# Two ways to bring the expert layer's output back to its tokens: scattered by token as it is made, or stored by slot and gathered at the end

## What is computed

```python
logits = flat @ router_w
_, topk_idx = top_k(logits + router_bias, K)            # K = 4 of E = 64 experts
topk_scores = softmax(logits) at topk_idx, divided by their sum
comb[token, topk_idx] = topk_scores
g = silu(einsum('nd,edf->nef', flat, wg))               # F = 64
u = einsum('nd,edf->nef', flat, wu)
routed = einsum('ne,nef,efd->nd', comb, g * u, wd)
shared = silu(flat @ swg) * (flat @ swu) @ swd          # the shared network, hidden width 512
return routed + shared
```

## Time and profile before

| | us |
|---|---|
| median of 3 runs (lowest, highest) | 1531.79 (1531.74, 1532.27) |
| the profiled execution, first to last instruction | 1770.5 |
| PE busy in it | 1348.5 (76%) |
| VectorE busy | 1091.4 (62%) |
| GpSimd busy | 921.4 (52%) |
| ACT busy | 687.1 (39%) |

### The profile page before, as it was taken

How to read it: one execution, slowest core, us unless ns; L and a number is a source line. 1 busy time by engine, 2 the same in 40 slices (tenths; PEclk the granted TensorE clock), 3 DMA queues, 4 the chain that set the end, 5 groups by cost and what they waited for, 6 DMA issues and landing times. The chain is left out here.

```text
span 1770.5 us, 24406 instructions
## 1 busy us (share of the span) xinstructions
PE 1348.5 (76%) x7408; PEld 924.2 (52%) x7408; DVE 1091.4 (62%) x2773; ACT 687.1 (39%) x1466; POOL 921.4 (52%) x1063
## 2 busy tenths in 40 slices
PE   6686656788699986998688985638876777777775
PEld 2344523455588873564456564325544555555533
DVE  5899755556366662473777775725654655555558
ACT  5998201111366652424133613111214444544420
POOL 3999364554555546656636032663453555555520
PEclk9898577889899998999799997869888888888878
DMA  9800531121788876112111003521136444443168
GB/s 363 343 1 0 201 136 56 71 86 61 207 276 265 271 250 185 57 46 69 39 53 39 3 1 128 219 101 49 68 97 185 148 140 140 140 134 105 40 238 272
DMA packets 109395, 233.81 MB, mean 132 GB/s; under 512 B 21543, under 2 KB 43470, under 8 KB 108756
## 3 DMA queue, kind: packets, MB, share of 16 engines
q1 hardware_dynamic: 81076, 164.03, 27.6%
q0 software_dynamic: 27648, 68.23, 11.3%
q10 hardware_dynamic: 544, 0.00, 0.0%
HBM read 125.44 MB, written 115.11 MB: 136 GB/s over the span
## 5 line engine op out<-in xcount | busy, mean ns | idle before, releaser
L882 POOL DMA_INDIRECT slots_x<-arena,slot x256 | 258.2, 1009 | 207.7 <-DVEq L981 131.4
L1248 POOL DMA_INDIRECT pairs_y<-arena x192 | 189.1, 985 | 177.2 <-DVE arena L1319 117.4
L1167 PE MATMUL moe_narrow<-arena 128*128 128x128 f32 x1536 | 232.7, 301 | 8.0 <-DVE arena L1311 6.7
L1311 DVE TENSOR_TENSOR arena<-arena,moe_narrow 64x128 f32<-64x128 f32 x384 | 111.6, 291 | 205.2 <-ACT arena L1215 186.3
L1167 PEld LDWEIGHTS moe_narrow<-arena 128*128 128x128 f32 x1536 | 212.9, 215 | 16.7 <-issue 15.0
L1156 PE MATMUL moe_narrow<-ident,arena 128*128 128x128 f32 x768 | 137.7, 308 | 92.8 <-ACT arena L1209 68.3
L707 PE MATMUL moe_wide<-arena 128*128 128x512 f32 x384 | 190.7, 644 | 22.0 <-DVE arena L1002 22.0
L1209 ACT ACTIVATE arena<-moe_narrow 128x512 f32<-128x512 f32 x192 | 114.6, 597 | 197.7 <-remote 117.8
L456 POOL DMA_INDIRECT arena<-slots_y,slot x128 | 128.7, 1005 | 87.0 <-DMA arena<-slots_y,slot 46.6
L1156 PEld LDWEIGHTS moe_narrow<-ident,arena 128*128 128x128 f32 x768 | 93.7, 155 | 146.8 <-issue 143.8
L799 ACT ACTIVATE arena<-moe_wide 128x512 f32<-128x512 f32 x48 | 28.7, 598 | 319.0 <-PE moe_wide L707 153.7
(11 more groups left out here) (318 smaller groups left out, 2410.4 us busy)
## 6 DMA issues: line engine op xcount, KB each, us to landing
arena<-slots_x SPq DMA_DIRECT2D x192, 264.0 KB, 3.8
slots_x<-arena SPq DMA_DIRECT2D x48, 528.0 KB, 15.8
slots_y<-arena SPq DMA_DIRECT2D x96, 256.0 KB, 3.7
arena<-w_gu SPq DMA_DIRECT2D x2, 8192.0 KB
arena<-pairs_y SPq DMA_DIRECT2D x32, 512.0 KB, 5.7
residual<-x SPq DMA_DIRECT2D x8, 512.0 KB
arena<-sw_gu SPq DMA_DIRECT2D x4, 1024.0 KB
slots_x<-arena,slot POOLq DMA_INDIRECT x256
```

What stands on the lines that cost most here:

```text
L882: pool.indirect_dma_start(out=x_slots, in_=xn[:, t, :], in_offset=None, out_offset=bass.IndirectOffsetOnAxis(ap=slot[:, t, i:i + 1], axis=0))\
L1167: last = pe.matmul(h_ps[n % 2][:, j * P:(j + 1) * P], weights[:, n % 3, j, h, :], xt[:, n % XTRING, (j * KH + h) * P:(j * KH + h + 1) * P] ...
L1248: pool.indirect_dma_start(out=slots.y_of, in_=ytile[:, n % YRING, j, :], in_offset=None, bounds_check=slots.pairs - 1, oob_is_err=False, o ...
```

## The change

Three things change in the second expert layer. Its experts stage takes the form of the first layer's: y is stored by slot by SP, GpSimd copies weights, and `scatters`, the targets and `pairs_y` are gone from the kernel. In the final sum GpSimd gathers the rows of `slots_y`, each gather `apart` from the one two before. And FB is 4 there, so four blocks of the shared network run in the final sum; the output is stored by pairs of tiles. In both layers the rows of `slots_x` lose their tail: 256 numbers instead of 264. The routing loop runs over TURNS = 6 turns, as it has to with fewer early blocks.

```diff
-        self.x = nc.dram_tensor("slots_x", (self.tiles * P, width + self.TAIL), F32, kind="Internal").ap()
+        self.x = nc.dram_tensor("slots_x", (self.tiles * P, width), F32, kind="Internal").ap()
         self.y = nc.dram_tensor("slots_y", (self.tiles * P, width), F32, kind="Internal").ap()
-        self.y_of = nc.dram_tensor("pairs_y", (self.pairs, width), F32, kind="Internal").ap()
...
-    def load(self, sp, t):
-
-        self.free(sp, t)
-        rows = self.k.slots.y_of.rearrange("(t p i) d -> t p i d", p=P, i=self.K)
-        sp.dma_start(self.ring[:, t % self.G], rows[t]).then_inc(self.sem(f"in{t % self.G}_0"), 16)
...
-                for parity in range(min(self.transfers, 2)):
-                    transfers = self.transfers // 2 if self.transfers > 1 else 1
-                    dve.wait_ge(self.sem(f"in{place + j}_{parity}"), 16 * transfers * turn + 16 * transfers)
+                for parity in range(2):
+                    dve.wait_ge(self.sem(f"in{place + j}_{parity}"), 16 * (self.K // 2) * (turn + 1))
...
-            for n in range(FB):
+            for n in range(TURNS):
                 a = n + AHEAD
-                gate_up(n, 2)
+                if n < FB:
+                    gate_up(n, 2)
                 if a < NB:
                     transposes(a, 0)
-                gate_up(n, 3)
+                if n < FB:
+                    gate_up(n, 3)
                 if a < NB:
                     transposes(a, 1)
                 if n + 1 < FB:
                     gate_up(n + 1, 0)
                 if a < NB:
...
-    XRING, XTRING, YRING, RING = (8, 2, 4, 8) if scatters else (5, 3, 4, 8)
-    HTRING = 3 if scatters else 4
...
+    XRING, XTRING, YRING, RING, HTRING = 5, 3, 4, 8, 4
...
-            if scatters:
-                for n in range(XRING, NP):
-                    load(n)
-            else:
-                for s in range(NP + DOWN):
-                    if s + XRING < NP:
-                        load(s + XRING)
-                    if s >= DOWN:
-                        store(s - DOWN)
-                for at in range(YRING):
-                    sp.wait_ge(exp_sem(f"y_out{at}"), Y_LANDED * NP // YRING)
+            for s in range(NP + DOWN):
+                if s + XRING < NP:
+                    load(s + XRING)
+                if s >= DOWN:
+                    store(s - DOWN)
+            for at in range(YRING):
+                sp.wait_ge(exp_sem(f"y_out{at}"), 16 * NP // YRING)
...
-                elif s > DOWN and (s - DOWN) % 2:
+                if s > DOWN and (s - DOWN) % 2:
...
-            if scatters:
-                for n in range(NP):
-                    if n % 2 == 0:
-                        pool.wait_ge(exp_sem("targets"), n // 2 + 1)
-                    pool.wait_ge(exp_sem("y_kept"), n + 1)
-                    for j in range(2):
-                        pool.indirect_dma_start(
-                            out=slots.y_of, in_=ytile[:, n % YRING, j, :], in_offset=None, bounds_check=slots.pairs - 1,
-                            oob_is_err=False, out_offset=bass.IndirectOffsetOnAxis(
-                                ap=goes_to[:, 2 * n + j:2 * n + j + 1], axis=0))\
-                            .then_inc(exp_sem(f"y_out{n % YRING}"), 16)
-                hand_over(pool, "y")
-                return
             held = {}
...
-            def find_targets(n):
-
-                for i in range(2):
-                    dve.wait_ge(exp_sem(f"x_in{(n + i) % XRING}"), 16 * ((n + i) // XRING + 1))
-                tails = xin[:, n % XRING:n % XRING + 2, :, D:].rearrange("p s t d -> p (s t) d")
-                here = every_expert[:, 2 * n:2 * n + 4].unsqueeze(2).to_broadcast([P, 4, K])
-                steps.link(dve.tensor_tensor(hits, tails[:, :, 0:K], here, ALU.is_equal))
-                steps.link(dve.tensor_tensor(hits, hits, tails[:, :, K:2 * K], ALU.mult))
-                steps.link(dve.tensor_reduce(target, hits, AX_X, ALU.add))
-                steps.link(dve.tensor_scalar(goes_to[:, 2 * n:2 * n + 4], target, float(slots.NOWHERE), None, ALU.add))
-                dve.sem_inc(exp_sem("targets"), 1)
-
             def multiply(n):
...
                 sp.dma_start(late_sd, sw_d.rearrange("(j p) n -> p j n", p=P)).then_inc(sum_sem("shared_w"), 16)
-            for at in range(YRING):
-                sp.wait_ge(exp_sem(f"y_out{at}"), Y_LANDED * NP // YRING)
+            view = out.rearrange("b (t p) c -> p (b t) c", p=P)
+            for pair in range(SUMMED):
+                tiles = slice(2 * pair, 2 * pair + 2)
+                sp.wait_ge(sum_sem("added"), 2 * K * (pair + 1))
+                if pair >= PAIRS * FB:
+                    sp.wait_ge(sum_sem("down_read"), pair - PAIRS * FB + 1)
+                sp.dma_start(view[:, tiles, :], k.res[:, tiles, :]).then_inc(sum_sem("stored"), 16)
+            sp.wait_ge(sum_sem("stored"), 16 * SUMMED)
+
+        def sum_gpsimd(pool):
             for t in range(sum_tiles):
-                choices.load(sp, t)
-            view = out.rearrange("b (t p) c -> p (b t) c", p=P)
-            for n in range(NB):
-                tiles = slice(BLK * n, BLK * (n + 1))
-                sp.wait_ge(sum_sem("added"), 2 * K * PAIRS * (n + 1))
-                sp.dma_start(view[:, tiles, :], k.res[:, tiles, :]).then_inc(sum_sem("stored"), 16)
-            sp.wait_ge(sum_sem("stored"), 16 * NB)
+                choices.gather(pool, t, apart=True)
...
-            assert FB == 6 and PAIRS == 2
+            assert PAIRS == 2 and SH == 4 and 2 * LATE + 2 <= SUMMED
             for pair in range(SUMMED):
+                if 2 * pair < SH * LATE:
+                    multiply(2 * pair)
+                if PAIRS <= pair < PAIRS * (LATE + 1):
+                    add_down(pair // PAIRS - 1, pair % PAIRS)
+                if 2 * pair < SH * LATE:
+                    multiply(2 * pair + 1)
                 add_choices(pair)
-                if 1 <= pair <= SH * LATE:
-                    multiply(pair - 1)
-                if pair == 6:
-                    add_down(0, 0)
-                if 9 <= pair <= 11:
-                    add_down((pair - 8) // 2, (pair - 8) % 2)
...
             experts_gpsimd(pool)
+            if sum_tiles:
+                sum_gpsimd(pool)
...
-        experts(nc, k, "moe2", 2, True, 6, k.res.shape[1], router_w, router_bias, w_gu, w_d, sw_gu, sw_d, out=out, first=first)
+        experts(nc, k, "moe2", 2, 4, k.res.shape[1], router_w, router_bias, w_gu, w_d, sw_gu, sw_d, out=out, first=first)
```

More of the change, by code:

```diff
@@ L489, in settled, with experts @@
         dve.wait_ge(self.sem("added"), 2 * self.K * (pairs - self.first // 2))
-def experts(nc, k, phase, turn, scatters, early, sum_tiles, router_w, router_bias, w_gu, w_d, sw_gu, sw_d, out=None, first=None):
+def experts(nc, k, phase, turn, early, sum_tiles, router_w, router_bias, w_gu, w_d, sw_gu, sw_d, out=None, first=None):
     NT, D = k.res.shape[1], k.res.shape[2]
@@ L578, in experts @@
     ytile = arena.take(YRING, 2, D)
-    if scatters:
[L580 to L585, removed]
+    assert arena.at <= arena.floats
     G = 8
@@ L756, in route_tensor @@
                     logits(a)
-                down(n, 0)
+                if n < FB:
+                    down(n, 0)
                 if n + 1 < FB:
@@ L761, in route_tensor @@
                     rank(a)
-                down(n, 1)
+                if n < FB:
+                    down(n, 1)
             pe.wait_ge(sem("tp_full"), KH * NB)
@@ L821, in route_scalar @@
             silu(0, 1)
-            for n in range(FB):
+            for n in range(TURNS):
                 a = n + AHEAD
-                silu(n, 2)
+                if n < FB:
+                    silu(n, 2)
                 if a < NB:
                     keep_transposes(a, 0)
-                silu(n, 3)
+                if n < FB:
+                    silu(n, 3)
                 if a < NB:
@@ L927, in choose @@
                 steps.settled()
-                choice = xn[:, BLK * n:BLK * (n + 1), D:D + K] if scatters else choices_of
-                steps.link(dve.tensor_copy(choice, which[:, :, 0:K]))
+                steps.link(dve.tensor_copy(choices_of, which[:, :, 0:K]))
                 steps.link(dve.tensor_tensor(by_choice,
                                              k.iota64[:, 0:E].unsqueeze(1).unsqueeze(1).to_broadcast([P, BLK, K, E]),
-                                             choice.unsqueeze(3).to_broadcast([P, BLK, K, E]), ALU.is_equal))
+                                             choices_of.unsqueeze(3).to_broadcast([P, BLK, K, E]), ALU.is_equal))
                 steps.link(dve.tensor_tensor(sums, by_choice[:, :, 0, :], by_choice[:, :, 1, :], ALU.add))
@@ L1056, in route_vector @@
                 statistics(7)
-            for n in range(FB):
+            for n in range(TURNS):
                 a = n + AHEAD
-                if n:
+                if 1 <= n <= FB:
                     add_down(n - 1, 1)
-                multiply(n, 2)
```

(26 more changed lines are left out.)

62 lines of the change are left out of this document (17 added, 45 removed).

## The result

The changed kernel takes 1616.79 us (median of 4 runs, 1612.83 to 1619.24) against 1532.03 us (1531.74 to 1536.08): a ratio of 1.0537, with a 95% interval of 1.0514 to 1.056. It is 5.4% slower; 4.5% was forecast, and 1616.8 lies in the range of 1552 to 1622. Sign and size came out; not every term did, and two of the misses cancel.

The account below looks back on a forecast made before the run. GpSimd's issue rate was taken to bound the old experts stage in timed runs; 1531.8 - 65.6 (experts) + 143.1 (sum) - 3 (routing) - 4 (narrow rows) = 1602 us, stated as 1600, 4.5% slower; range 1552 to 1622.

Parts of the forecast that it names:

- The old experts stage in a timed run: Second layer's experts stage before the change: bound by GpSimd's issue of 192 scatters, 267 us instead of the profile's 365.
- the stops: Unnamed waits of ACT, some 5.6 us each, beside dense indirect transfers in the profile; timed runs have next to none.
- the seven intervals from 1500.19 to 1509.35: Stretch of scatters in the old experts stage's timeline, given as support for 1.285 us per scatter.
- The balance: Losses of 131.4 us in routing, 95.5 in second experts stage, 22 in retention: 249, against 238.7 between profile and runs.
- The new experts stage: Second layer's experts in the first layer's form: 201.4 us, saving 65.6 us in timed runs, 163.7 against the profile.
- Rival B: Stops are in the timed runs too, so the experts stage gives back its whole 163.7 us: 1495 us; chance 0.13.
- The sum: Second layer's final sum: 128 uncovered gathers instead of 32 plain loads, 213.6 us against 70.5, so 143.1 us more.
- I take 1.6 us: Interval between gathers in the final sum, each waiting for the landing of the one two before: 127 x 1.6 = 203.2 us.
- Rival A: Final sum's gathers held by issue alone at 1.26 us, landing wait never binding: sum 43 us shorter, 1558 us; chance 0.12.
- Rival C: VectorE's adds slow the gathers' issue in the final sum: it grows by 50 us, to 1650 us; chance 0.05.
- Four early blocks: Two shared-network blocks leave second-layer routing, which GpSimd's scatters bound: at most 1 us each comes free, 3 us in all.
- Narrow rows: x rows of 1024 instead of 1056 bytes: indirect issues every 1.25 instead of 1.265 us, 4 us over 256 scatters.

Follow-up runs that it names:

- The third scatter: The kernel before with a third scatter per pair, of the same rows, into a spare tensor that nobody reads: 1658.85 us, 1.0816 of before.

## Why the prediction was right, and where it was not

**The old experts stage in a timed run: 267 us forecast, 267.6 measured.** The step was to set GpSimd's issue rate against the stops and take the stops out. The third scatter and the profile of the unchanged kernel show it. The terms came as 18.2 us to the first scatter (19.5 forecast), 247.3 for 191 intervals (245.4) and 2.2 (2.2). One reading beside them was off: the seven intervals from 1500.19 to 1509.35 give 1.309 us each and not 1.285; 1.295 was measured over the whole stage.

**The stops belong to the profiled execution only.** The size was right. Set against the new profile, the old one is longer by 60.4 and 60.1 us in the two routings (first scatter to first x load), by 19.8 from the first layer's gathers to the second routing, and by 97.5 in the second experts stage: 237.8 of the 238.6 us between them. The balance had 131.4 for the routings (17.3 of these waits are in the new profile too), 22 and 95.5. The reading "only the profiled execution pays them" holds for that execution, not for profiling: the same program profiled again has none, and nor have the ten other kernels here. What made them is open; no run brought them back. The forecast that the profile would get shorter while the runs get longer came true against the profile shown, for the reason of that odd execution.

**The new experts stage: 201.4 us forecast, 197.2 measured**; the saving is 70.4 us instead of 65.6. Rival B, the side where the change gains, falls with the 267.6: the old stage keeps none of its 98 us of stops.

**The sum: 213.6 us forecast, 227.2 measured**, against 71.4 before. This is the term that was mis-sized most: "I take 1.6 us" became 1.716, over 127 intervals 14.7 us. With one gather in flight the interval is 3.18 us, and 1.59 would be its half; the pairs don't overlap evenly, and 1.65, the mean that stood in the earlier trace rows, was the better price.

**Rival A** (issue alone, 1558 us) is false for the changed kernel: 80.0 us of waits for landings. But its price is near that of the version without the wait, which takes 1559.71 us. **Rival C** did not come: the mean issue of the gathers in the sum is 973 ns, with VectorE's adds beside them.
The Trainium skill's box on VectorE locking GpSimd out ("SBUF — State Buffer", the "DVE blocks DMA" trap) speaks of two-port operations and names fp32 copies; whether it holds for these adds of two inputs, it does not say. The 973 ns show no such lock for this kind of add.

**Four early blocks: 3 us forecast,** 3.4 measured between the two profiles (182.9 to 179.5 us), some 3 from six to four blocks alone. **Narrow rows: 4 us forecast, nothing found.** The scatter's median issue is 960 ns with either width, and routing with six blocks takes 182.6, 182.6 and 183.0 us in three profiles with rows of 1024 bytes and 182.9, 182.5 and 182.9 in three with 1056. The difference that I read between two lines was the difference between a gather (0.946 us) and a scatter (0.960).

Summed over the two profiles: -70.4 (experts), +155.8 (sum), -3.4 (routing), -2.8 (all that stands ahead of the second routing): +79.2 us, which is 1611.1 - 1531.9. The forecast had +70.5. The sum cost 12.7 us more than forecast; the experts stage gave 4.8 more and the narrow rows 4 less, and these two nearly cancel, which is luck. The medians of the runs lie further apart than the two profiles, by 84.8 us: the profiled execution was the fastest of the changed kernel.

No version tried that computes the right output beats the kernel before. The gain of the new experts stage, 70 us, is less than the gathers cost even at the issue rate: the sum without the wait takes 173.6 us, 102 more than plain loads. The scatters cost about the same issue time each, but 192 of them lay beside 197 us or more of other work; the 128 gathers, 165 us at 1.29, lie beside a stage that takes only 71 to 73 us with plain loads.

## What to carry to other kernels

Before pricing a change from a trace, set its span against the runs: where it is far longer, look which stretches can hold the difference, or profile again. Work of an issue-bound engine is cheap where it lies beside another stage, and costs its full rate where it stands alone: count what it covers, not how many it issues. A wait for the n-th transfer before sets an interval of about the landing time over n, as long as that is more than the issue takes; and removing a long wait uncovers what its neighbours had in line behind it.

## What the runs showed of the hardware that was not expected

Indirect gathers of 128 rows of 1 KB from GpSimd come every 3.18 us with one in flight, 1.716 with two, 1.309 with four and 1.294 without a limit. Scatters of the same size, up to 288 in a row with one each 1.29 us, came with no unnamed stop of another engine in eleven profiles, while one execution of the kernel before had 22 such stops of ACT, of 5.6 us in the mean, in its second experts stage alone; their cause is open.
